# First attention of a four-layer kernel: probabilities normalised in ACT's cast, keys and values split on GpSimd, key halves placed by DMA

## The chip, the cores and the metric

One Trainium2 chip, one of its cores. The metric is the time of one execution on the device in microseconds; several executions are taken and their median is given. Engines are named as in the profile: PE (tensor engine, matmuls), ACT (scalar engine), DVE (vector engine), POOL (GpSimd), SP (the engine that issues most DMAs here).

## The reference, cut to what matters

Four layers, each followed by a residual sum and a layer norm: an attention with relative positions, a mixture of experts (top 2), a second attention, a second mixture with fixed capacity. The change is in the first, over 8 batches of 512 tokens of 128 features, 16 heads of 64:

```python
q, k, v = jnp.einsum('bsx,xAnh->Abnsh', input, w)
q = q + q_bias[:, None, :]
a = jnp.einsum('bnqh,bnkh->bnqk', q, k) * h ** (-0.5)
...
pos_scores = jnp.einsum('bnqh,nvh->bnqv', q, emb) * h ** (-0.5)
a = a + relative_causal(pos_scores)
mask = jnp.tril(jnp.ones((s, s), dtype=bool))
a = jax.nn.softmax(jnp.where(mask, a, NEG_INF), axis=-1)
o = jnp.einsum('bnqk,bnkh->bqnh', a, v).reshape(b, s, n * h)
...
out = o @ (out_kernel * (fan_in * fan_out) ** (-0.25)) + out_bias
```

## The kernel before, in words

The phase is `rel_attention_phase` (from L303). Each engine has its own program, and they meet by semaphores only. `schedule` (L333) gives every engine the same order: 64 bodies, one for each pair of heads n of a batch (8 pairs in each of 8 batches), with `k` alternating between 0 and 1 for double buffers; some bodies stand in loops over registers. The order within a body is written out by hand for each engine.

Products are taken in three float16 passes (high by high, low by high, high by low), so each operand is split: the high part is a cast to float16, the low part is the float32 value less the high part. The relative positions are folded into the score product: rows 0 to 63 of a head's 128 contraction rows are the head's q and k, rows 64 to 127 (for head 1 the other way round) hold fixed tables in `m.k_h`, `m.k_l` and projected q.

What a body does for the pair n, by engine:

- PE (`body` at L502): scores of head 0 (n) into three banks `score_ps`, projection of k for n+1 into `kv_ps`, projection of q of head 0 for n+1 into `q_ps`, `weighted_values` for n-2, scores of head 1, q of head 1, projection of v for n (again `kv_ps`), and the output projection for n-2. `weighted_values` (L458) first broadcasts the reciprocals of the row sums by eight float32 matmuls against the identity into `r_ps` (L466), then multiplies transposed probabilities and values (L476).
- ACT (L568): exponentials of head 0 with row sums (`exps`, L541), between them the copy of k out of PSUM with its scale (`k_copy`, L566), the cast of the unnormalised probabilities (128 x 1280) times `P_SCALE` to float16 (`high`, L550), the copy of `r_ps` (`r_copy`, L554), exponentials of head 1, the high part of v (`v_high`, L560), the cast of head 1.
- DVE (L644): maxima of head 0 (L594), reciprocals and low part of head 1 of the pair before (L602, L606), `q_evac` of head 0 for n+1 (bias and factor, L612), low part of head 0, `normalise` for n-2 (weighted values times reciprocals, L619), reciprocals of head 0, maxima of head 1, `q_evac` of head 1, low part of v (L623). At the last pair of a batch it adds the output bias to the residual (L628) and normalises the batch before (L123); at the third pair it sums that batch (L634).
- POOL (L711): four splits for n+1, in the order k of head 0 (64 partitions), q of head 0, k of head 1, q of head 1. A split is a one-column operation as a gate (L130), the high part (L691, an affine_select that writes float16) and the low part (L694). k is written into its 64 rows of `m.k_h` and `m.k_l`. At the last pair of a batch it computes the inverse deviation (L136, L137).
- SP (L406): issues the transposes of the float16 probabilities (`turn`, L404), head 1 of the pair before, then head 0 of this one, each when its low part is done.

Scores of head 1 wait for the exponentials of head 0 bank by bank, as the three score banks are shared, and those of head 0 for head 1's of the pair before. `kv_ps` is shared by k and v: the next k projection waits for `v_lo`, the v projection for `k_out`.

## Time and profile before

| what | value |
|---|---|
| median of 3 runs | 1677.52 us (1674.55 to 1745.03) |
| the profiled execution | 1676.82 us |
| its span in the profile | 1675.1 us |
| mean PE clock over the span | 0.948 of full |
| the first attention | from about 37 to 798 us of the span |

The profile has one record for each instruction. The page gives totals; windows give busy time within a stretch; the timeline gives instructions in order, with the idle time ahead of one and what released it in square brackets; waits are those idle times added up by waiter and releaser. "Busy" leaves out the time in which an instruction waits for a semaphore, but an instruction that has started and is held by something else counts as busy. Matmuls overlap in the records (their ends are modelled), so a busy PE need not be a saturated one. Times are us, means in the groups ns.

### The profile page before, as it was taken

How to read it: one execution, taken by the hardware profiler on the slowest of the kernel's cores; microseconds unless marked ns; L12 is line 12 of the kernel's file. 1: busy time of each engine (PE TensorE's matmuls, PEld its weight loads, DVE VectorE, ACT ScalarE, POOL GpSimd, SP SyncE). 2: the span in 40 equal slices, each digit the busy share in tenths (PEclk: the TensorE clock that was granted, in tenths of full speed). 3: DMA queues.
4: the chain of work that ended last, by engine and by line, in shares of the span. 5: the costliest groups of instructions: out<-in, count | busy, mean ns of one | idle time of the engine just before them, and what ended most of it. 6: DMA issues, size and time to landing. Idle time of an engine off the chain costs nothing. (4 is left out here: it accounts for less than half of the span.)

```text
span 1675.1 us, 38178 instructions
## 1 busy us (share of the span) xinstructions
PE 1421.9 (85%) x12519; PEld 834.2 (50%) x12519; DVE 1262.4 (75%) x2722; ACT 971.0 (58%) x1921; POOL 879.9 (53%) x1203
## 2 busy tenths in 40 slices
PE   4899989898998999897589887489899899898736
PEld 3566666666666666665356555123333333332216
DVE  3788888887888888886688888377787787777534
ACT  2677767676776767675244443156666666665431
POOL 2877778777787777775445555211221221222524
PEclk9899999999999999999699999599999999999977
DMA  5645545454454545544000000411011011010001
GB/s 160 123 113 127 123 98 125 97 122 110 110 125 105 114 111 118 116 110 94 0 2 0 0 0 0 146 48 35 27 39 36 26 39 36 26 40 28 13 12 27
DMA packets 372881, 116.47 MB, mean 70 GB/s; under 512 B 341675, under 2 KB 369312, under 8 KB 372704
## 3 DMA queue, kind: packets, MB, share of 16 engines
q1 hardware_dynamic: 369472, 111.36, 27.9%
q10 hardware_dynamic: 1824, 3.15, 0.6%
q0 software_dynamic: 1536, 1.34, 0.3%
q8 instruction: 27, 0.44, 0.1%
q14 instruction: 22, 0.18, 0.0%
HBM read 20.36 MB, written 12.89 MB: 20 GB/s over the span
## 5 line engine op out<-in xcount | busy, mean ns | idle before, releaser
L541 ACT ACTIVATE prob<-score_ps,nmax 128x512 f32<-128x512 f32 (+3 forms) x512 | 264.9, 526 | 209.0 <-DVE nmax L594 209.0
L1563 DVE TENSOR_REDUCE a_nm<-a_s 128x1 f16<-128x512 f32 x512 | 324.8, 687 | 55.5 <-PE a_s L1335 53.6
L1489 ACT ACTIVATE a_pt<-a_st 128x1024 f32<-128x1024 f32 x256 | 260.4, 1021 | 131.4 <-PE a_st L1353 116.3
L130 POOL TENSOR_TENSOR gate<-mhalf 128x1 f32<-128x1 f32 (+1 forms) x284 | 124.2, 437 | 259.3 <-ACT k L566 137.6
L1335 PE MATMUL a_s<-a_kop,a_qop 128*128 128x512 f16 x512 | 199.6, 391 | 64.2 <-DVE a_nm L1563 47.4
L606 DVE SCALAR_TENSOR_TENSOR p<-prob,p 128x1280 f16<-128x1280 f32 x128 | 204.6, 1598 | 49.8 <-ACT p L550 49.8
L594 DVE TENSOR_REDUCE nmax<-score_ps 128x1 f32<-128x512 f32 (+3 forms) x512 | 213.0, 475 | 3.4 <-PE score_ps L455 3.3
L452 PE MATMUL score_ps<-k_h,q_h 128*128 128x512 f16 (+3 forms) x512 | 158.2, 309 | 22.4 <-ACT prob L541 14.2
L550 ACT ACTIVATE p<-prob 128x1280 f16<-128x1280 f32 x128 | 163.8, 1279 | 6.5
L888 ACT ACTIVATE hid<-fps,b_cols 128x512 f32<-128x512 f32 x130 | 86.3, 687 | 127.2 <-PE fps L848 127.2
L694 POOL TENSOR_TENSOR q_l<-q,q_h 128x512 f16<-128x512 f32 x130 | 152.9, 1176 | 10.8
L454 PE MATMUL score_ps<-k_h,q_l 128*128 128x512 f16 (+3 forms) x512 | 156.9, 306 | 0.0
L453 PE MATMUL score_ps<-k_l,q_h 128*128 128x512 f16 (+3 forms) x512 | 156.7, 306 | 0.0
L694 POOL TENSOR_TENSOR k_l<-k,k_h 64x512 f16<-64x512 f32 x130 | 150.1, 1154 | 10.8
L1353 PE MATMUL a_st<-a_qop,a_kop 128*128 128x512 f16 x512 | 153.4, 383 | 0.2
L984 POOL TENSOR_TENSOR hid_l<-hid,hid_h 128x512 f16<-128x512 f32 x65 | 97.2, 1495 | 107.1 <-DVE hid_h L952 107.1
L1335 PEld LDWEIGHTS a_s<-a_kop,a_qop 128*128 128x128 f16 x512 | 50.8, 99 | 191.0 <-DVE a_nm L1563 156.0
L1366 PE MATMUL a_pv<-a_pt,a_vaug 128*32 128x512 f32 x1024 | 138.3, 612 | 0.7 <-ACT a_pt L1489 0.7
L476 PE MATMUL pv_ps<-pt,v_h 128*64 128x256 f16 (+1 forms) x1536 | 116.9, 256 | 0.3 <-DMA pt<-p 0.3
L455 PE MATMUL score_ps<-causal,ident_bf 128*128 128x128 bf16 x512 | 114.1, 223 | 0.0
L1685 POOL TENSOR_TENSOR a_vaug<-a_v,a_bv 128x128 f32<-128x128 f32 x32 | 14.4, 455 | 185.8 <-PE a_pv L1366 130.9
L862 PE MATMUL fps<-w_h,hid_h 128*128 128x128 f16 (+1 forms) x512 | 93.0, 221 | 21.0 <-POOL hid_l L984 19.4
(331 smaller groups left out, 3433.5 us busy)
## 6 DMA issues: line engine op xcount, KB each, us to landing
a_qop<-q_parts SPq DMA_DIRECT2D x32, 128.0 KB
a_kop<-k_parts SPq DMA_DIRECT2D x128, 24.0 KB
x_tok<-in_L_attn_input_dram SPq DMA_DIRECT2D x4, 512.0 KB, 12.3
pt<-p SPq DMA_TRANSPOSE x128, 4.1
e_w<-in_L_ffn_w_dram SPq DMA_DIRECT2D x1, 2048.0 KB, 8.3
q_parts<-a_q_h SPq DMA_DIRECT2D x16, 128.0 KB
k_parts<-a_k_h SPq DMA_DIRECT2D x16, 128.0 KB
out_dram<-a_res SPq DMA_DIRECT2D x8, 256.0 KB
```

The source lines that it names most:

```text
L452: nc.tensor.matmul(o, q_h[h][:, qs], m.k_h[h][:, 0:w], start=True, stop=False)
L453: nc.tensor.matmul(o, q_h[h][:, qs], m.k_l[h][:, 0:w], start=False, stop=False)
L454: nc.tensor.matmul(o, q_l[h][:, qs], m.k_h[h][:, 0:w], start=False, stop=False)
L541: ins = nc.scalar.activation(prob[h][:, P_OFF[c]:P_OFF[c] + w], score_ps[u][:, col:col + w], ACT.Exp, bias=nmax[h][:, c:c + 1], accum_out= ...
L550: nc.scalar.activation(p16[h][k][:, 0, :], prob[h][:, :], ACT.Copy, scale=P_SCALE).then_inc(p_hi[h], 1)
L594: ins = nc.vector.tensor_reduce(nmax[h][:, c:c + 1], score_ps[u][:, col:col + P * (c + 1)], AX.X, ALU.max, negate=True)
L606: nc.vector.scalar_tensor_tensor(p16[h][k][:, 1, :], prob[h][:, :], P_SCALE, p16[h][k][:, 0, :], ALU.mult, ALU.subtract).then_inc(p_lo[h], 1)
L694: return nc.gpsimd.tensor_tensor(lo, src, hi, ALU.subtract)
L1335: nc.tensor.matmul(s_ps[k][:, :], qop[:, g, c * P:(c + 1) * P], kop[:, hh, g, :], start=True, stop=True).then_inc(s_mm[k], 1)
L1353: mm = nc.tensor.matmul(st_ps[r][:, i, :], kop[:, 2 * r + i, g, kc * P:(kc + 1) * P], qop[:, g, :], start=True, stop=True)
L1489: nc.scalar.activation(pt[kc % 2][r][:, :, :], st_ps[r][:, :, :], ACT.Exp, scale=1.0 / SC).then_inc(exp_done[r], 1)
L1563: nc.vector.tensor_reduce(nm[g % 2][:, c, hh:hh + 1], s_ps[c % 2][:, :], AX.X, ALU.max, negate=True).then_inc(max_done[c % 2], 1)
```

## The change

`P_SCALE` becomes 64, and the probabilities are normalised before they are cast, so nothing is divided behind the weighted values:

- DVE's `reciprocals` also multiplies by `P_SCALE`, in an instruction of its own. ACT's `high` waits for it and casts in four pieces, one for each block of rows with its own factor per partition; DVE's `low` does the same in four pieces.
- The eight matmuls into `r_ps` go, and `normalise`; `r_copy` becomes `o_copy`, a copy of `pv_ps` to `o32`. The freed bank gives q a bank per head.
- `v_high` becomes `v_copy` (float32), and both parts of v are made on POOL (`split_v`). `v_low` goes.
- POOL splits the keys of both heads in one split of 128 partitions into `k16`, and SP places each half into `m.k_hl[h]` with a DMA (`place_k`), 64 partitions of 2 KB.
- The orders within a body change on ACT, DVE, POOL and SP. In the FFN phase one semaphore is saved.

```diff
-P_SCALE = 1024.0
+P_SCALE = 64.0
...
+            def place_k(h, n):
+                sp.wait_ge(k_split, n + 1)
+                sp.sem_inc(turn_open, 1)
+                sp.wait_ge(s_mm[h], 3 * n)
+                r = slice(64 * h, 64 * h + 64)
+                sp.dma_start(m.k_hl[h][r, :, :], k16[r, :, :]).then_inc(k_in[h], 16)
...
             def body(n, t, b, p, k):
                 if later(n, 1):
                     turn(1, n - 1, 1 - k)
+                place_k(0, n + 1)
                 turn(0, n, k)
+                place_k(1, n + 1)
...
             def scores(h, n):
                 pe.wait_ge(q_split[h], n + 1)
-                pe.wait_ge(k_split[h], n + 1)
+                pe.wait_ge(k_in[h], 16 * (n + 1))
...
             def high(h, n, t, k):
-                act.wait_ge(exp_done[h], count(n, 2))
+                act.wait_ge(r_done[h], n + 1)
                 if later(n, 2):
                     act.wait_ge(turned[h][k], 16 * t)
-                nc.scalar.activation(p16[h][k][:, 0, :], prob[h][:, :], ACT.Copy, scale=P_SCALE).then_inc(p_hi[h], 1)
+                for c in range(QC):
+                    cs = slice(P_OFF[c], P_OFF[c] + P * (c + 1))
+                    ins = nc.scalar.activation(p16[h][k][:, 0, cs], prob[h][:, cs], ACT.Copy, scale=rsum[h][:, c:c + 1])
+                ins.then_inc(p_hi[h], 1)
...
             def body(n, t, b, p, k):
-                exps(0, n, [0, 1])
+                exps(0, n, [0, 1, 2])
                 k_copy(n + 1)
-                exps(0, n, [2])
                 high(0, n, t, k)
                 if later(n, 2):
-                    r_copy(n - 2)
+                    o_copy(n - 2)
                 exps(1, n, [0, 1, 2])
-                v_high(n, k)
+                v_copy(n)
                 high(1, n, t, k)
...
-                nc.vector.reciprocal(rsum[k][:, :, h], sums[h][:, :]).then_inc(r_done[h], 1)
+                nc.vector.reciprocal(rsum[h][:, :], sums[h][:, :]).then_inc(r_steps, 1)
+                dve.wait_ge(r_steps, 2 * n + h + 1)
+                nc.vector.tensor_scalar(rsum[h][:, :], rsum[h][:, :], P_SCALE, None, ALU.mult).then_inc(r_done[h], 1)
...
-                nc.vector.scalar_tensor_tensor(p16[h][k][:, 1, :], prob[h][:, :], P_SCALE, p16[h][k][:, 0, :],
-                                               ALU.mult, ALU.subtract).then_inc(p_lo[h], 1)
+                dve.wait_ge(r_done[h], n + 1)
+                for c in range(QC):
+                    cs = slice(P_OFF[c], P_OFF[c] + P * (c + 1))
+                    ins = nc.vector.scalar_tensor_tensor(p16[h][k][:, 1, cs], prob[h][:, cs], rsum[h][:, c:c + 1], p16[h][k][:, 0, cs],
+                                                         ALU.mult, ALU.subtract)
+                ins.then_inc(p_lo[h], 1)
...
                 if later(n, 1):
-                    reciprocals(1, n - 1, 1 - k)
                     low(1, n - 1, 1 - k)
+                reciprocals(0, n)
                 q_evac(0, n + 1, pw)
                 if behind:
                     batch_stats(b - 1)
+                maxima(1, n)
                 low(0, n, k)
-                if later(n, 2):
-                    normalise(n - 2)
-                reciprocals(0, n, k)
-                maxima(1, n)
                 q_evac(1, n + 1, pw)
-                v_low(n, k)
+                reciprocals(1, n)
...
+            def split_k(n):
+                pool.wait_ge(k_out, n + 1)
                 for h in range(2):
-                    split_k(h, n)
-                    split_q(h, n)
+                    pool.wait_ge(k_in[h], 16 * n)
+                split(slice(0, P), k32[:, :], k16[:, 0, :], k16[:, 1, :], 4 * n + 1).then_inc(k_split, 1)
+
+            def split_v(n, k):
+                pool.wait_ge(v_out, n + 1)
+                if later(n, 2):
+                    pool.wait_ge(pv_mm, n - 1)
+                v = [t[k][:, :, :].rearrange("p c n -> p (c n)") for t in (v_h, v_l)]
+                split(slice(0, P), v32[:, :], v[0], v[1], 4 * n + 8).then_inc(v_split, 1)
...
             def body(n, t, b, p, k):
-                split_k(0, n + 1)
+                split_k(n + 1)
                 split_q(0, n + 1)
-                split_k(1, n + 1)
                 split_q(1, n + 1)
+                split_v(n, k)
```

## Rows read from the trace of the kernel before

**Rows 1.** The page: busy time, share and count of each engine over the span.

```profile
PE 1421.9 (85%) x12519; PEld 834.2 (50%) x12519; DVE 1262.4 (75%) x2722; ACT 971.0 (58%) x1921; POOL 879.9 (53%) x1203
```

**Rows 2.** Windows, one body: engine busy, then PE clock, DMA share, GB/s.

```profile
446.16:457.18 11.02, 10.50 (x115) 7.52 (x114) 9.00 (x17) 8.18 (x21) 8.67 (x13) 1.00 0.52 119
```

**Rows 3.** Waits in 100:740: waiter, releaser, total us, times, longest.

```profile
ACT prob L541 <- DVE nmax L594: 178.5, 111, 4.4
```

**Rows 4.** Timeline of DVE, one body: start, us, what, count [idle before].

```profile
445.44 1.67 DVE L594 TENSOR_REDUCE nmax<-score_ps 128x1 f32<-128x512 f32 x4
...
447.12 1.46 DVE L606 SCALAR_TENSOR_TENSOR p<-prob,p 128x1280 f16<-128x1280 f32 x1
...
450.21 1.69 DVE L606 SCALAR_TENSOR_TENSOR p<-prob,p 128x1280 f16<-128x1280 f32 x1 [0.97 <-ACT p L550]
...
452.51 1.65 DVE L594 TENSOR_REDUCE nmax<-score_ps 128x1 f32<-128x512 f32 x4
...
455.86 0.69 DVE L623 SCALAR_TENSOR_TENSOR v_l<-kv_ps,v_h 128x512 f16<-128x512 f32 x1 [1.05 <-ACT v_h L560]
456.47 0.68 DVE L594 TENSOR_REDUCE nmax<-score_ps 128x1 f32<-128x512 f32 x1
```

**Rows 5.** Timeline of ACT: key copies around a wrap, then one body.

```profile
398.97 0.60 ACT L566 ACTIVATE k<-kv_ps 128x512 f32<-128x512 f32 x1
...
414.20 0.60 ACT L566 ACTIVATE k<-kv_ps 128x512 f32<-128x512 f32 x1
...
447.74 0.60 ACT L566 ACTIVATE k<-kv_ps 128x512 f32<-128x512 f32 x1
...
448.91 1.27 ACT L550 ACTIVATE p<-prob 128x1280 f16<-128x1280 f32 x1
450.09 0.58 ACT L554 ACTIVATE r_sb<-r_ps 128x512 f32<-128x512 f32 x1
...
453.20 0.69 ACT L541 ACTIVATE prob<-score_ps,nmax 128x512 f32<-128x512 f32 x1 [2.53 <-DVE nmax L594]
...
455.22 0.61 ACT L560 ACTIVATE v_h<-kv_ps 128x512 f16<-128x512 f32 x1
```

**Rows 6.** Timeline of POOL, the same body: the operation ahead of a split.

```profile
448.57 0.19 POOL L130 TENSOR_TENSOR gate<-mhalf 64x1 f32<-64x1 f32 x1 [1.53 <-ACT k L566]
...
450.72 1.23 POOL L130 TENSOR_TENSOR gate<-mhalf 128x1 f32<-128x1 f32 x1 [0.17 <-POOL k_l L694]
```

**Rows 7.** Timeline of POOL and DVE at a wrap.

```profile
409.83 1.01 POOL L137 TENSOR_TENSOR ln_rstd<-ln_ve,mhalf 128x4 f32<-128x4 f32 x1
...
410.88 1.11 DVE L123 TENSOR_SCALAR x_tok<-ln_y,ln_mv,ln_rstd 128x128 f32 x4 [2.30 <-POOL ln_rstd L137]
```

**Rows 8.** Windows of line 466 alone, one body.

```profile
446.16:457.18 11.02, 1.09 (x16) 0.85 (x16) 1.00 0.52 119
```

**Rows 9.** Groups of ACT by form: count, busy us, mean ns, idle before.

```profile
L541 ACT ACTIVATE prob<-score_ps,nmax 128x512 f32<-128x512 f32 x128 | 87.9, 687 | 207.9 <-DVE nmax L594 207.9
...
L541 ACT ACTIVATE prob<-score_ps,nmax 128x128 f32<-128x128 f32 x128 | 46.6, 364 | 0.0
```

**Rows 10.** Timeline of POOL and DVE where they meet, and four pieces in a row.

```profile
438.37 1.15 POOL L694 TENSOR_TENSOR k_l<-k,k_h 64x512 f16<-64x512 f32 x1
...
438.71 2.16 DVE L606 SCALAR_TENSOR_TENSOR p<-prob,p 128x1280 f16<-128x1280 f32 x1 [0.37 <-ACT p L550]
...
799.54 3.75 POOL L990 TENSOR_SCALAR_AFFINE_SELECT w_h<-e_w 128x2048 f16<-128x2048 f32 x2 [1.46 <-SPq L733]
...
799.57 1.89 DVE L902 CAST wg_h<-wg_raw 128x8 f16<-128x8 f32 x1 [0.33 <-PEq L288]
...
870.87 1.12 DVE L961 SCALAR_TENSOR_TENSOR x_tok<-fps,comb,x_tok 128x128 f32 x4
```

**Rows 11.** DMA issues: tiles, queue, count, size, us to landing.

```profile
pt<-p SPq DMA_TRANSPOSE x128, 4.1
...
c_xe<-slot_rows SPq DMA_DIRECT2D x4, 162.5 KB, 3.8
```

More of the change, by code:

```diff
@@ L297, in rel_attention_phase @@
         k32 = sb("k32", [P, S], F32)
+        k16 = sb("k16", [P, 2, S], F16)
+        v32 = sb("v32", [P, S], F32)
         v_h = [sb(f"v_h{k}", [P, QC, P], F16) for k in range(2)]
@@ L306, in rel_attention_phase @@
         sums = [sb(f"sums{h}", [P, QC], F32) for h in range(2)]
-        rsum = [sb(f"rsum{k}", [P, QC, 2], F32) for k in range(2)]
+        rsum = [sb(f"rsum{h}", [P, QC], F32) for h in range(2)]
         y = sb("ln_y", [P, QC, D], F32)
@@ L313, in rel_attention_phase @@
         score_ps = [ps(f"score_ps{u}") for u in range(3)]
-        q_ps, kv_ps, pv_ps, r_ps, out_ps = ps("q_ps"), ps("kv_ps"), ps("pv_ps"), ps("r_ps"), ps("out_ps")
+        q_ps, pv_ps, out_ps = [ps(f"q_ps{h}") for h in range(2)], ps("pv_ps"), ps("out_ps")
+        kv_ps = ps("kv_ps")
         pair = lambda name: [sem(f"{name}{h}") for h in range(2)]
@@ L404, in turn, with first_front @@
                 sp.dma_start_transpose(pt[h][k][:, :, :], p16[h][k][:, :, :].rearrange("p a b -> p (a b)")).then_inc(turned[h][k], 16)
+            def place_k(h, n):
[4 more added lines that the diff above has]
+                sp.dma_start(m.k_hl[h][r, :, :], k16[r, :, :]).then_inc(k_in[h], 16)
+            def first_front():
+                place_k(0, 0)
+                place_k(1, 0)
             def body(n, t, b, p, k):
@@ L408, in body @@
                     turn(1, n - 1, 1 - k)
+                place_k(0, n + 1)
                 turn(0, n, k)
-            schedule(sp, lambda: None, body, lambda: turn(1, B * PAIRS - 1, 1))
+                place_k(1, n + 1)
+            schedule(sp, first_front, body, lambda: turn(1, B * PAIRS - 1, 1))
             sp.wait_ge(m.f0_loaded, m.F0_LOADS)
@@ L458, in weighted_values @@
             def weighted_values(n, t, k):
-                pe.wait_ge(r_done[1], n + 1)
                 if later(n, 1):
                     pe.wait_ge(o_done, n)
-                for c in range(QC):
-                    for h in range(2):
-                        nc.tensor.matmul(r_ps[64 * h:64 * h + 64, c * P:(c + 1) * P], rsum[k][:, c, h:h + 1].to_broadcast([P, 64]),
-                                         m.ident[:, :], start=True, stop=True)
-                pe.wait_ge(v_lo, n + 1)
+                pe.wait_ge(v_split, n + 1)
                 for h in range(2):
@@ L545, in high, with o_copy, v_copy @@
             def high(h, n, t, k):
[L547 removed]
+                act.wait_ge(r_done[h], n + 1)
                 if later(n, 2):
                     act.wait_ge(turned[h][k], 16 * t)
[L550 to L552 removed]
+                for c in range(QC):
+                    cs = slice(P_OFF[c], P_OFF[c] + P * (c + 1))
+                    ins = nc.scalar.activation(p16[h][k][:, 0, cs], prob[h][:, cs], ACT.Copy, scale=rsum[h][:, c:c + 1])
+                ins.then_inc(p_hi[h], 1)
+            def o_copy(n):
                 act.wait_ge(pv_mm, n + 1)
[L554 to L556 removed]
+                if later(n, 1):
+                    act.wait_ge(out_mm, n)
+                nc.scalar.activation(o32[:, :], pv_ps[:, :], ACT.Copy).then_inc(o_done, 1)
+            def v_copy(n):
                 act.wait_ge(v_mm, n + 1)
[L558 to L561 removed]
+                act.wait_ge(v_split, n)
+                nc.scalar.activation(v32[:, :], kv_ps[:, :], ACT.Copy, scale=W_SCALE).then_inc(v_out, 1)
             def k_copy(n):
                 act.wait_ge(k_mm, n + 1)
[L565 removed]
+                act.wait_ge(k_split, n)
                 nc.scalar.activation(k32[:, :], kv_ps[:, :], ACT.Copy, scale=W_SCALE * QK_SCALE).then_inc(k_out, 1)
             def body(n, t, b, p, k):
[L569 removed]
+                exps(0, n, [0, 1, 2])
                 k_copy(n + 1)
[L571 removed]
                 high(0, n, t, k)
                 if later(n, 2):
[L574 removed]
+                    o_copy(n - 2)
                 exps(1, n, [0, 1, 2])
[L576 removed]
+                v_copy(n)
                 high(1, n, t, k)
@@ L657, in body @@
                     batch_stats(b - 1)
+                maxima(1, n)
                 low(0, n, k)
-                if later(n, 2):
-                    normalise(n - 2)
-                reciprocals(0, n, k)
-                maxima(1, n)
                 q_evac(1, n + 1, pw)
-                v_low(n, k)
+                reciprocals(1, n)
                 if wrap:
@@ L676, in last @@
                 n = B * PAIRS
-                reciprocals(1, n - 1, 1)
                 low(1, n - 1, 1)
-                normalise(n - 2)
-                normalise(n - 1)
                 batch_sum(B - 1)
@@ L725, in last @@
                 layer_norm_gpsimd(nc, pool, m, B - 1, mv, ve, rstd)
-            schedule(pool, lambda: front(0), body, last)
+            schedule(pool, first_front, body, last)
 def moe_top2_phase(nc, io, m):
@@ L1980, in build @@
             m.wo = sb0("wo", [P, PAIRS, D], F32)
-            m.k_h = [sb0(f"k_h{h}", [P, S], F16) for h in range(2)]
-            m.k_l = [sb0(f"k_l{h}", [P, S], F16) for h in range(2)]
+            m.k_hl = [sb0(f"k_hl{h}", [P, 2, S], F16) for h in range(2)]
+            m.k_h, m.k_l = ([t[:, part, :] for t in m.k_hl] for part in range(2))
             m.q_mult = sb0("q_mult", [P, 2, S], F32)
```

66 lines of the change are left out of this document (21 added, 45 removed).

## The prediction

> **What bounds the kernel now.** The engine totals come first: no engine is full over the span, the tensor engine is nearest with 85% [rows 1]. They mix five phases, and the change lies in one, the first attention. So one of its bodies comes next: of 11.02 us PE is busy 10.50, DVE 9.00, ACT 8.18, POOL 8.67 (with PE's clock at 1.00 in this stretch) [rows 2]. In that phase the longest wait of all is ACT's for DVE's maxima [rows 3]. PE is fuller than the others, yet whether it sets the pace is not told by its share.
>
> The ring can be read off one body. DVE: maxima of head 0 from 445.44, low part of head 1 at 447.12, low part of head 0 at 450.21 after an idle 0.97 for ACT's cast, maxima of head 1 at 452.51, value low part at 455.86 after an idle 1.05 for ACT's value copy, next maxima at 456.47 [rows 4]. ACT: key copy 447.74, cast 448.91, exponentials of head 1 at 453.20, value copy 455.22 [rows 5]. So it runs DVE maxima, ACT exponentials with the key copy among them, ACT cast, DVE low and normalise, DVE maxima, ACT exponentials, value copy, DVE value low: 11.03 us, and DVE goes from one wait for ACT to the next. It is a ring of hand-overs between DVE and ACT; PE, 0.5 short of full, only fits into it. POOL needs 9.5 of the 11.02 and stands idle 1.53 before each key split [rows 6]. Once per batch a body takes 15.23 (key copies at 398.97 and 414.20) [rows 5]: DVE waits 2.30 for POOL's deviation and has a norm of 1.11 to do [rows 7]. The steady bodies start 11.02 or 11.03 apart.
>
> **The change part by part.** The sum is made against the profiled execution, 1676.8 (span 1675.1 and 1.7 around it), 0.7 under the median of 1677.5.
>
> *Removed from PE.* The sixteen passes that broadcast the reciprocals, 1.09 us per body [rows 8]. PE falls to about 9.4, so it is no bound under 9.4. Alone that is worth nothing, as PE isn't in the ring; bounds 0 and its wait-free share, 1.09.
>
> *Removed from DVE.* Normalise is what lies between the end of the low part at 450.21 (1.69 long) and the maxima at 452.51, 0.6 with a small reciprocal; the value low part is 456.47 less 455.86, 0.61 [rows 4]: 1.2 per body, both in the ring. The second q bank removes a cross wait that costs nothing now.
>
> *ACT's cast becomes four casts with a per-partition scale.* One cast of 1280 takes 1.27 [rows 5]: 1.08 is the stream (exponentials of 512 against 128 columns: 687 less 364 ns for 384, so 0.84 ns each [rows 9]), 0.2 is fixed. A per-partition operand costs 0.087 (exponential of 512 with its bias 687 [rows 9], key copy without one 600 [rows 5]). The cast at 448.91 is followed by the copy at 450.09, 0.09 before its end [rows 5], so pieces overlap by that. Four pieces: 1.08 + 4 x (0.2 + 0.087 - 0.09) = 1.9, plus 0.7 per head. Bounds: 1.38 if the fixed cost is paid once, 2.27 without overlap. I take 1.90, as the rows show each term. The Trainium skill ("ScalarE: Activation LUTs", section "What ACT_TABLE_LOAD costs") gives 186 ns fixed, 93 ns per pointer operand and 93 ns overlap back to back; by its figures the four would last 1.90, an estimate, and the rows agree.
>
> *DVE's low part becomes four.* The one instruction took 1.46 undisturbed (447.12) [rows 4], the next 0.08 before its end. Four scalar_tensor_tensors of 128 columns with pointer scalars take 1.12 at 870.87 [rows 10]: 0.27 each, 0.13 of it over a stream of about 1.04 ns a column (1.33 for 1280). So 1.33 + 4 x 0.13 = 1.85 instead of 1.38. Bounds 1.4 (nothing per piece) and 2.3 (the whole 0.27 over each).
>
> *Reciprocals.* A multiply and a self-wait are added, two each per body: some 0.4 instead of 0.1 to the release (three hand-overs and two instructions of 0.1 each; bounds 0.2 and 0.6); ACT now waits for it before each cast. On ACT the key copy or value copy (0.48) covers it if DVE is free.
>
> *The ACT ring without collisions.* Exponentials 2 x 2.02 (453.20 to 455.22), three copies of 0.48, two casts of 1.90, four hand-overs of 0.1: 4.04 + 1.44 + 3.80 + 0.40 = 9.7. DVE's work: maxima 2 x 1.6 (445.44 to 447.12, less a small reciprocal) [rows 4], low 2 x 1.85, q_evac 2 x 0.68 (what the 9.00 leaves for it), reciprocals 2 x 0.4 = 9.1. POOL: four splits as before (the second key's half is replaced by the value's), each 2.15 (448.57 to 450.72) [rows 6]: 8.6. So 9.7 would be the body, if nobody met anybody.
>
> *They do meet.* DVE's low part and POOL exclude each other, the whole instruction long. The low part at 438.71 took 2.16 instead of 1.46 because POOL's key low part ran until 439.52; a cast of eight columns took 1.89 behind POOL's select at 799.54 [rows 10]. The other way round POOL's gate took 1.23 instead of 0.19 behind the low part, 1.04 lost [rows 6]. Today one low part falls into POOL's 1.53 idle and only one collides. In the new order:
> - POOL's second q split needs q_evac(1), which DVE runs behind low(0); then comes the value split, 2.15 later. ACT's cast(1) starts 0.5 after q_evac(1) and lasts 1.90. So the value split starts just as low(1) does, always. Four pieces give POOL's 1.15 subtraction a boundary to enter at (DVE likewise gets in between two POOL operations at 799.57 [rows 10]); low(1) then ends after some 0.5 (the high part first) + 1.85 + 1.1 = 3.4, and reciprocals(0) behind it is 1.2 late against the exponentials' end at 2.1: plus 1.15.
> - The multiply in the reciprocals reads and writes SBUF alone, as the cast at 799.57 does, so it can wait for a POOL operation of up to 1.15. I take 0.3 per body, bounds 0 and 2.3.
> - Low(0) comes behind cast(0), while POOL splits key and q(0) without a pause; it waits for the rest of a 1.15 subtraction or is split by one: half of that and a little, plus 0.65, bounds 0 and 2.
>
> Body: 9.7 + 1.15 + 0.3 + 0.65 = 11.8, against 11.02. The Trainium skill ("SBUF — State Buffer", section "Who interferes with whom") says that a DVE instruction with two SBUF inputs contends with a GpSimd instruction that reads SBUF, and a one-source copy or tensor_scalar in a two-port mode as well, as an exclusive lock; the trace agrees for the low part (2.16 against 1.46), while no row has a tensor_scalar beside POOL. Without that rule the body would be 9.7 by the sum.
>
> *Keys by DMA.* Two more DMAs of 128 KB per body on SP's queue. A transpose lands 4.1 after its issue; place_k(0) is issued behind turn(1), place_k(1) behind turn(0). A plain DMA of 162.5 KB lands in 3.8 here [rows 11], which I take as the bound above.
>
> Half 0: key copy, 2.15 for the split, 3.8 for the DMA, so at most 6.0 after the key copy; scores and DVE's next maxima(0) come 0.9 later, and DVE gets there some 7.3 after the key copy. Hidden. Half 1: in a body that starts with the exponentials, low(0) ends at about 8.9, its transpose lands at 13.0, the half between 13.0 and 16.8. The next key split wants to start at 11.8 + 2.6 = 14.4. I take 14.0 (the DMA's way lies mostly beside the transpose), cost 0, bounds 0 and 2.4.
>
> *Batch edges.* Seven wraps. The deviation (1.01 and a small sum) [rows 7] now stands behind q(1) and the value split on POOL: 2 x 2.15 + 1.2 + 0.2 = 5.7 after q_evac(1), then DVE's norm 1.1 and the first maximum 0.7: exponentials 7.5 after q_evac(1), 2.4 in a plain body, plus 5.1. Statistics between q_evac(0) and maxima(1) put about 1.1 in the ring (taken as long as the norm). Together 6.2 over a body, now 15.23 - 11.02 = 4.2: plus 2.0 x 7 = 14; bounds 0 and 25.
>
> **Sum.** 63 steps between 64 bodies: 1676.8 + 63 x (11.8 - 11.02) + 14 = 1676.8 + 49 + 14 = **1740**. With every term at its lower bound PE's 9.4 would hold (about 1580), at the upper ones a body passes 14 (over 1850); neither end is likely in all terms at once.
>
> **The rivals.**
> - *Faster: the collisions mostly miss.* For it: 1.53 of idle on POOL today, and DVE's own 2.0. Against it: the value split is tied to low(1) by q_evac(1). Body 10.1 (9.7 and 0.4 for what is left): 1676.8 - 58 + 14 = 1633. Chance 0.25.
> - *Same: half of them.* The multiply isn't held and low isn't split by POOL: body 11.0, 1676.8 + 0 + 14 = 1690. Chance 0.2.
> - *My forecast*, body 11.8, own range 1705 to 1780. Chance 0.45.
> - *Slower still: key halves late.* Place: SP's queue behind turn(0). It decides once half 1 lands over 5.5 us behind the issue of that transpose (8.9 to 14.4); POOL's key split starts late and q, scores, maxima follow. At 6.5 the body is 12.8: 1676.8 + 112 + 14 = 1803. Chance 0.1.
>
> A measurement of this kernel can tell about 2%, 1644 and 1711. Faster 0.25, same 0.24 (the second rival and the lower edge of my range), slower 0.51. The range 1630 to 1800 takes in the first rival's time and ends short of the last's.
>
> **What would show it.** Right: bodies about 11.8 apart; the four casts 1.9 long; ACT waiting for reciprocals (DVE) ahead of casts; low pieces of over 1 us among shorter ones; POOL gates over 0.3; a wrap of 18. Wrong: bodies under 10.5 with ACT nearly full (no collisions), casts of 1.4 in sum (the fixed cost was mis-sized), or POOL's key gate waiting for a DMA (the keys' way is the bound).

## The result and the profile after

| what | before | after |
|---|---|---|
| median | 1676.16 us, 4 runs (1674.55 to 1745.03) | 1744.89 us, 4 runs (1743.88 to 1747.28) |
| ratio after/before | | 1.0415, 95% interval 1.0395 to 1.0436 |
| profiled execution, span | 1676.82, 1675.1 | 1747.28, 1745.6 |
| mean PE clock over the span | 0.948 | 0.934 |

The change makes the kernel 4.1% slower. 1740 was predicted, in a range of 1630 to 1800. The ratios leave out executions in a slower state of the chip: the 1745.03 above and one of 1984.39 in an experiment below.

The page of the changed kernel, its engine totals and the two groups that carry the new casts and low parts (count, busy us, mean ns of one, idle before):

```profile
PE 1370.0 (78%) x11495; PEld 785.6 (45%) x11495; DVE 1386.7 (79%) x3106; ACT 1046.7 (60%) x2305; POOL 823.0 (47%) x1201
...
L621 DVE SCALAR_TENSOR_TENSOR p<-prob,rsum,p 128x128 f16<-128x128 f32 (+3 forms) x512 | 364.3, 770 | 11.6 <-ACT p L563 11.6
...
L563 ACT ACTIVATE p<-prob,rsum 128x128 f16<-128x128 f32 (+3 forms) x512 | 245.6, 550 | 149.8 <-DVE rsum L614 149.8
```

Against [rows 1] PE has lost 52 us and DVE has gained 124, though it has shed `normalise` and the low part of v. The 512 low pieces take 770 ns in the mean, where four that nothing disturbs take 1.94 together (seen in two experiments below), under 500 each. So DVE's growth is in the low parts. ACT's casts are 550 ns in the mean, four of them 1.92 with their overlap, and 150 us of idle time stands ahead of them, all of it for DVE's `rsum`. Where ACT waited for DVE's maxima [rows 3], it now waits for the reciprocals:

The waits of the changed kernel from 100 to 780 us (waiter, releaser, total us, times, longest):

```profile
POOL gate L130 <- DVE q L628: 139.8, 56, 3.0
ACT p L563 <- DVE rsum L614: 129.0, 111, 2.1
...
PE score_ps L469 <- DMA k_hl<-k: 63.3, 78, 3.2
```

The first two are for DVE; the last one shown is for the keys' way over the DMA (PE's weight loads wait another 25.3 for them), and whether it matters is tried below. The window of one body answers to [rows 2] (its length, then busy time of PE, PE's weight loads, DVE, ACT and POOL, then clock, DMA share, GB/s):

```profile
472.26:483.95 11.69, 9.73 (x99) 6.65 (x97) 11.49 (x23) 9.34 (x28) 7.92 (x13) 1.00 0.61 136
```

The body has grown from 11.02 to 11.69, and DVE is busy 11.49 of it (11.03 to 11.45 in the next five), where it had been 9.00. Its timeline, one body from low part to low part, shows with what. A row of x4 holds four pieces and names the shape of the first:

```profile
472.39 3.21 DVE L621 SCALAR_TENSOR_TENSOR p<-prob,rsum,p 128x128 f16<-128x128 f32 x4 [0.37 <-ACT p L563]
...
475.71 0.51 DVE L614 TENSOR_SCALAR rsum<-rsum 128x4 f32<-128x4 f32 x1
...
478.39 2.74 DVE L621 SCALAR_TENSOR_TENSOR p<-prob,rsum,p 128x128 f16<-128x128 f32 x4
...
481.91 0.18 DVE L614 TENSOR_SCALAR rsum<-rsum 128x4 f32<-128x4 f32 x1
482.02 1.69 DVE L606 TENSOR_REDUCE nmax<-score_ps 128x1 f32<-128x512 f32 x4
```

POOL at the same time:

```profile
472.27 0.61 POOL L690 TENSOR_SCALAR_AFFINE_SELECT v_h<-v 128x512 f16<-128x512 f32 x1
472.97 1.16 POOL L693 TENSOR_TENSOR v_l<-v,v_h 128x512 f16<-128x512 f32 x1
475.08 0.56 POOL L130 TENSOR_TENSOR gate<-mhalf 128x1 f32<-128x1 f32 x1 [0.96 <-ACT k L580]
475.60 0.61 POOL L690 TENSOR_SCALAR_AFFINE_SELECT k<-k 128x512 f16<-128x512 f32 x1
...
481.88 0.19 POOL L130 TENSOR_TENSOR gate<-mhalf 128x1 f32<-128x1 f32 x1 [2.48 <-DVE q L628]
```

The reader is to see three things. The value split (472.27 to 474.13) stands inside the low part of head 1 (472.39 to 475.60), which takes 3.21. The low part of head 0 takes 2.74; it starts inside q's subtraction, which runs from 478.24 to 479.40. And the multiply at 475.71 takes 0.51 where its sister at 481.91 takes 0.18: it starts inside the select at 475.60 and ends with it. The same view over a window of 0.1 us gives single pieces:

```profile
472.95 1.45 DVE L621 SCALAR_TENSOR_TENSOR p<-prob,rsum,p 128x256 f16<-128x256 f32 x1
...
478.39 1.16 DVE L621 SCALAR_TENSOR_TENSOR p<-prob,rsum,p 128x128 f16<-128x128 f32 x1
```

Undisturbed these two take 0.48 and 0.35 (in the experiment with the thin value split, at 507.61 and 507.34). The first is the second piece of low(1), held while the value subtraction runs (472.97 to 474.13). The other is the first piece of low(0), held to the end of q's subtraction. So POOL enters low(1) at a boundary between two pieces, while low(0) only waits once, at its start.

With starts instead of lengths, since instructions overlap by 0.08, the body is: four undisturbed terms of DVE (maxima 2 x 1.59, low 2 x 1.86, q_evac 2 x 0.66, reciprocals 2 x 0.30) 8.82, waits and hand-overs 0.47, and 2.40 of collisions (1.26 in low(1), 0.81 in low(0), 0.33 in the multiply).

Once per batch, where [rows 7] show a wait of 2.30 for the deviation:

```profile
453.05 0.74 DVE L628 SCALAR_TENSOR_TENSOR q<-q_ps,q_bias,q_mult 128x512 f32<-128x512 f32 x1
...
459.41 1.12 DVE L123 TENSOR_SCALAR x_tok<-ln_y,ln_mv,ln_rstd 128x128 f32 x4 [4.24 <-POOL ln_rstd L137]
```

The wait is 4.24. The key copies tell the length of every step; here the first two, and the ones around this wrap:

```profile
38.21 0.60 ACT L580 ACTIVATE k<-kv_ps 128x512 f32<-128x512 f32 x1
70.03 0.60 ACT L580 ACTIVATE k<-kv_ps 128x512 f32<-128x512 f32 x1
...
445.90 0.59 ACT L580 ACTIVATE k<-kv_ps 128x512 f32<-128x512 f32 x1
463.19 0.61 ACT L580 ACTIVATE k<-kv_ps 128x512 f32<-128x512 f32 x1
474.27 0.60 ACT L580 ACTIVATE k<-kv_ps 128x512 f32<-128x512 f32 x1
485.96 0.59 ACT L580 ACTIVATE k<-kv_ps 128x512 f32<-128x512 f32 x1
```

The wrap is 17.29 (it was 15.24), the step behind it 11.08 and a plain one 11.69. The first step is 31.82, where the kernel before took 9.74: a loss that the prediction does not have. The queue of SP and DVE's first maximum say why:

```profile
36.92 1.45 SPq L366 DMA_DIRECT2D e_w<-in_L_ffn_W_dram  x2
...
60.70 0.43 SPq L380 DMA_DIRECT2D a_bo<-in_L_attn_bo_dram  x1
61.26 1.21 SPq L415 DMA_DIRECT2D k_hl<-k  x2
...
66.39 0.69 DVE L606 TENSOR_REDUCE nmax<-score_ps 128x1 f32<-128x512 f32 x1 [25.36 <-PE score_ps L472]
```

SP first issues the loads of later phases' weights, 24 us of them, and the halves of the first keys stand behind. DVE's first maximum comes at 66.39; before it came at 44.08.

From the first key copy to the last are 64 steps. They sum to 732.9 before and 801.8 after:

| steps | before | after | more | predicted |
|---|---|---|---|---|
| the first | 9.7 | 31.8 | 22.1 | 0 |
| the next 15 | 165.8 | 178.8 | 13.0 | 12 |
| 48 (six groups of eight, each with a wrap) | 557.4 | 591.2 | 33.8 | 49 |

### The profile page after: what moved, and what is told of

It reads as the page before. It is cut to its first block and busy times, and to the rows that moved or that the text cites. A ratio compares the mean times of both kernels' runs of the same rounds, so it can differ in the third digit from the quotient of the medians.

```text
span 1745.6 us, 37368 instructions
## 1 busy us (share of the span) xinstructions
PE 1370.0 (78%) x11495; PEld 785.6 (45%) x11495; DVE 1386.7 (79%) x3106; ACT 1046.7 (60%) x2305; POOL 823.0 (47%) x1201
## 3 DMA queue, kind: packets, MB, share of 16 engines
q0 software_dynamic: 1536, 1.34, 0.3%
## 5 line engine op out<-in xcount | busy, mean ns | idle before, releaser
L621 DVE SCALAR_TENSOR_TENSOR p<-prob,rsum,p 128x128 f16<-128x128 f32 (+3 forms) x512 | 364.3, 770 | 11.6 <-ACT p L563 11.6
L563 ACT ACTIVATE p<-prob,rsum 128x128 f16<-128x128 f32 (+3 forms) x512 | 245.6, 550 | 149.8 <-DVE rsum L614 149.8
L552 ACT ACTIVATE prob<-score_ps,nmax 128x512 f32<-128x512 f32 (+3 forms) x512 | 260.1, 516 | 61.4 <-DVE nmax L606 61.3
L469 PE MATMUL score_ps<-k_hl,q_h 128*128 128x512 f16 (+3 forms) x512 | 160.1, 313 | 145.2 <-DMA k_hl<-k 98.6
L130 POOL TENSOR_TENSOR gate<-mhalf 128x1 f32<-128x1 f32 x283 | 74.4, 263 | 387.6 <-DVE q L628 159.3
L471 PE MATMUL score_ps<-k_hl,q_l 128*128 128x512 f16 (+3 forms) x512 | 159.5, 312 | 0.0
L470 PE MATMUL score_ps<-k_hl,q_h 128*128 128x512 f16 (+3 forms) x512 | 159.4, 311 | 0.0
L469 PEld LDWEIGHTS score_ps<-k_hl,q_h 128*128 128x128 f16 x512 | 51.5, 101 | 193.6 <-ACT prob L552 91.5
L505 PE MATMUL out_ps<-wo,o 128*128 128x128 f32 (+1 forms) x512 | 74.5, 289 | 36.2 <-ACT o L570 36.1
```

Source lines behind the costliest of these rows:

```text
L469: nc.tensor.matmul(o, q_h[h][:, qs], m.k_h[h][:, 0:w], start=True, stop=False)
L470: nc.tensor.matmul(o, q_h[h][:, qs], m.k_l[h][:, 0:w], start=False, stop=False)
L471: nc.tensor.matmul(o, q_l[h][:, qs], m.k_h[h][:, 0:w], start=False, stop=False)
L552: ins = nc.scalar.activation(prob[h][:, P_OFF[c]:P_OFF[c] + w], score_ps[u][:, col:col + w], ACT.Exp, bias=nmax[h][:, c:c + 1], accum_out= ...
L563: ins = nc.scalar.activation(p16[h][k][:, 0, cs], prob[h][:, cs], ACT.Copy, scale=rsum[h][:, c:c + 1])
L621: ins = nc.vector.scalar_tensor_tensor(p16[h][k][:, 1, cs], prob[h][:, cs], rsum[h][:, c:c + 1], p16[h][k][:, 0, cs], ALU.mult, ALU.subtract)
```

## The experiments

All are built from the changed kernel, but for the last. They ran on chips on which the kernel before takes 1664.4 to 1665.2; there the changed kernel takes 1664.5 x 1.0415 = 1733.6 by its ratio. "Body" is the usual distance of key copies. Two theories stood against each other: the body is set by DVE's low parts and POOL's splits excluding each other (mine, with ACT's ring as the base); or by what was added as plain work (longer casts, more instructions), or by the keys' way over a DMA.

### The first keys ahead of the loads

```diff
+            place_k(0, 0)
+            place_k(1, 0)
             load(m.w1_raw[:, :, :], ...)
```

> The changed kernel with the first two key halves' DMAs issued ahead of SP's weight loads instead of behind them. Theory (first keys wait for SP's queue of loads at the start, where the first maxima come at 66.4 us instead of 44.1): the first maxima near 44, the second body still late since its keys stand behind the loads; in all 12 to 20 us less, about 1729. Rival (the start is covered later, as the loop catches up): no change. The steady body stays at 11.69 under both.

Measured: 1724.65, ratio 1.0365 (1.0334 to 1.0395), 9 less than the changed kernel. The first step is 9.45, but the second is 28.1: the second pair's key halves still stand behind the loads, which only moved the stall by a body. So the place was right, and what this edit gives was overrated. Spreading the loads comes below.

### q_evac of head 1 ahead of the low part of head 0

```diff
                 maxima(1, n)
+                q_evac(1, n + 1, pw)
                 low(0, n, k)
-                q_evac(1, n + 1, pw)
```

> The changed kernel with DVE's q_evac of head 1 ahead of the low part of head 0. Theory of collisions: POOL's second q split follows the first without a wait, the value split follows at the value copy and is over before the low part of head 1 starts; that low part falls from 3.2 to about 2 us, the body from 11.69 to 10.3 to 10.8, the time to 1660 to 1690. Rival (the four-piece casts and low parts alone make the ring longer, collisions cost nothing): body unchanged within 0.2, since the same instructions stand on every engine.

Measured: 1816.63, ratio 1.0917 (1.0886 to 1.0949), body 13.69; a miss. The low part of head 1 is indeed free now, but its neighbour and POOL are not. DVE and POOL of this kernel:

```profile
485.95 1.94 DVE L621 SCALAR_TENSOR_TENSOR p<-prob,rsum,p 128x128 f16<-128x128 f32 x4 [0.41 <-ACT p L563]
...
493.69 3.19 DVE L621 SCALAR_TENSOR_TENSOR p<-prob,rsum,p 128x128 f16<-128x128 f32 x4
```

```profile
488.65 0.19 POOL L130 TENSOR_TENSOR gate<-mhalf 128x1 f32<-128x1 f32 x1 [3.47 <-DMA k_hl<-k]
```

And its waits, from 100 to 780 us:

```profile
POOL gate L130 <- DMA k_hl<-k: 151.8, 43, 5.0
...
PE score_ps L469 <- DMA k_hl<-k: 131.6, 54, 4.4
```

The low part is 1.94 without company. But POOL waits up to 5.0 for a half of the keys: the half of head 1 is issued behind the transpose of head 0, that behind low(0), and low(0) is now later. That is the last rival of the prediction (key halves late), with a body of 13.7 instead of its 12.8. It does not hold in the changed kernel, where POOL waits for a key half 5 times in this window, 10.0 in all, but it is near.

### The value split cut to a thirty-second

```diff
-                split(slice(0, P), v32[:, :], v[0], v[1], 4 * n + 8).then_inc(v_split, 1)
+                pool_gate(nc, m, slice(0, P))
+                nc.gpsimd.affine_select(out=v[0][:, 0:16], in_=v32[:, 0:16], ...)
+                nc.gpsimd.tensor_tensor(v[1][:, 0:16], v32[:, 0:16], v[0][:, 0:16], ALU.subtract)
```

> The changed kernel with POOL's value split cut to 16 of 512 columns (the rest of both value parts stays zero, so 31/32 of the values are left out). Theory of collisions: the low part of head 1 no longer meets a 0.61 and a 1.15 us POOL operation, it falls from 3.2 to about 2, the body to 10.4 to 10.6, the time to about 1675. Rival (piece costs alone): body 11.6 to 11.7, the time within 10 us of 1745.

Measured: 1688.12 (one execution), body 11.06, 0.63 less; 10.4 to 10.6 had been expected, so a miss in size. DVE:

```profile
501.38 3.01 DVE L621 SCALAR_TENSOR_TENSOR p<-prob,rsum,p 128x128 f16<-128x128 f32 x4
...
507.34 1.94 DVE L621 SCALAR_TENSOR_TENSOR p<-prob,rsum,p 128x128 f16<-128x128 f32 x4 [0.37 <-ACT p L563]
```

Low(1) has fallen from 3.21 to 1.94, so the value split is what meets it, as predicted. The body got only half of the 1.27: low(0) has grown from 2.74 to 3.01, as the splits of key and q now lie otherwise against it, and 0.3 went into the maxima of head 1 (1.85 instead of 1.67) and waits ahead of q_evac.

### The low part in one instruction again

```diff
-                for c in range(QC):
-                    ...
-                    ins = nc.vector.scalar_tensor_tensor(p16[h][k][:, 1, cs], prob[h][:, cs], rsum[h][:, c:c + 1], ...)
-                ins.then_inc(p_lo[h], 1)
+                nc.vector.scalar_tensor_tensor(p16[h][k][:, 1, :], prob[h][:, :], rsum[h][:, 0:1], ...).then_inc(p_lo[h], 1)
```

> The changed kernel with DVE's low part in one instruction with the first block's factor for all four (so the low parts of three row blocks are computed with another block's factor). Theory of collisions: a whole instruction waits at most once for POOL and isn't entered by it; low parts of 1.5 to 2.6 us instead of 2.7 to 3.2, body 10.2 to 10.6, time about 1665. Rival (only the fixed cost per piece counts): 0.4 less per low part, body 10.9, time about 1695.

Measured: 1669.12 (one execution), bodies of 10.05 and 11.16 in turn, 10.61 in the mean: a hit. Two bodies' low parts:

```profile
483.96 2.33 DVE L619 SCALAR_TENSOR_TENSOR p<-prob,rsum,p 128x1280 f16<-128x1280 f32 x1
...
494.40 1.84 DVE L619 SCALAR_TENSOR_TENSOR p<-prob,rsum,p 128x1280 f16<-128x1280 f32 x1 [0.15 <-ACT p L563]
...
499.54 1.72 DVE L619 SCALAR_TENSOR_TENSOR p<-prob,rsum,p 128x1280 f16<-128x1280 f32 x1
```

In these two bodies it takes 1.72 to 2.36 where the four pieces took 2.74 and 3.21; over the run it takes 1.54 to 2.51. Two things come off: the three more pieces (0.40 per low part, 1.94 against the 1.54 of a whole one that meets nobody, as at 72.42), and POOL's entries between them; each low part still meets POOL, but once. The body gains 1.08 of some 1.8 that the two low parts lose, as DVE now waits for others (its maxima at 482.19 for PE, 1.12).

This run also shows a reciprocal and the multiply behind it, both beside one subtraction of POOL (74.52 to 75.67):

```profile
74.54 0.17 DVE L612 RECIPROCAL rsum<-sums 128x4 f32<-128x4 f32 x1
...
74.74 0.95 DVE L614 TENSOR_SCALAR rsum<-rsum 128x4 f32<-128x4 f32 x1
```

The multiply is held to the end of the subtraction, the reciprocal is not.

### The cast in one instruction again

```diff
-                for c in range(QC):
-                    ...
-                    ins = nc.scalar.activation(p16[h][k][:, 0, cs], prob[h][:, cs], ACT.Copy, scale=rsum[h][:, c:c + 1])
+                nc.scalar.activation(p16[h][k][:, 0, :], prob[h][:, :], ACT.Copy, scale=rsum[h][:, 0:1])
```

> The changed kernel with ACT's cast in one instruction with the first block's factor for all four (the high parts of three row blocks get another block's factor). The cast falls from 1.92 to about 1.37. If ACT sets the pace, the body falls by 1.1 to 10.6 (time 1676). If DVE with its waits for POOL sets it (it is busy 11.49 of 11.69 with those waits counted), the casts lie beside DVE's work and the body falls by 0.6 or less, time 1708 to 1745.

Measured: 1719.21 (one execution), body 11.39 in the mean, 0.3 less. ACT and DVE of it:

```profile
485.82 1.36 ACT L561 ACTIVATE p<-prob,rsum 128x1280 f16<-128x1280 f32 x1 [1.42 <-DVE rsum L611]
```

```profile
482.07 2.75 DVE L618 SCALAR_TENSOR_TENSOR p<-prob,rsum,p 128x128 f16<-128x128 f32 x4
...
487.52 3.18 DVE L618 SCALAR_TENSOR_TENSOR p<-prob,rsum,p 128x128 f16<-128x128 f32 x4
```

The two casts have become 2 x 0.56 shorter and the body 0.3, which is about the 0.37 that DVE had stood idle for a cast. The low parts are as long as before, and ACT stands idle 1.42 ahead of a cast. So ACT's casts are not what sets the body; DVE is. This is what had been expected of that case (0.6 or less).

### Without the multiply

```diff
-                nc.vector.reciprocal(rsum[h][:, :], sums[h][:, :]).then_inc(r_steps, 1)
-                dve.wait_ge(r_steps, 2 * n + h + 1)
-                nc.vector.tensor_scalar(rsum[h][:, :], rsum[h][:, :], P_SCALE, None, ALU.mult).then_inc(r_done[h], 1)
+                nc.vector.reciprocal(rsum[h][:, :], sums[h][:, :]).then_inc(r_done[h], 1)
```

> The changed kernel without the multiply of the reciprocals and without the wait ahead of it (the probabilities are scaled by 1 instead of 64). The two instructions and waits take 0.2 to 0.5 each. Theory: body 11.69 less 0.4 to 0.7, time about 1705 to 1720. Rival (they lie beside ACT's copies): body unchanged.

Measured: 1710.56 (one execution), 23 less, bodies of 11.2 to 11.3: a hit. Two multiplies had cost 0.2 each in plain work and the one 0.33 more when held; 0.48 of it comes off a plain body, 0.40 off the mean of the 48 steps.

### The second key half ahead of the transpose

```diff
                 place_k(0, n + 1)
+                place_k(1, n + 1)
                 turn(0, n, k)
-                place_k(1, n + 1)
```

> The changed kernel with SP issuing the second key half ahead of the transpose of head 0 instead of behind it. PE waited 88.6 us in all for the key halves in the window 100:780. Theory (these waits are covered, PE isn't in the ring): time within 5 us of 1745, and PE's waits for the keys nearly gone. Rival (keys' way is in the ring): body 0.5 to 1 shorter, time 1685 to 1715.

Measured: 1733.38, ratio 1.0414 (1.0393 to 1.0435), body 11.71. The wait, from 100 to 780 us:

```profile
PE score_ps L469 <- DMA k_hl<-k: 34.8, 38, 2.2
```

PE's wait for keys falls from 63.3 to 34.8, that of its weight loads goes from 25.3 to 28.3, and the time does not move. The time is a hit, but the waits were expected to be nearly gone, and 63.1 of 88.6 are left. They are covered too: DVE, which sets the body, stands idle for scores only 8.2 in this window of the changed kernel. So the rival of late keys is out.

### Loads spread, with q_evac early

The loads of later phases are queued, eight behind each of the first bodies, and the first keys are placed ahead of all; q_evac as above.

```diff
-                sp.dma_start(dst, src, ...).then_inc(m.a_loaded, 16)
+                queued.append((dst, src, scattered))
...
                 place_k(1, n + 1)
+                for _ in range(8):
+                    if queued:
+                        dst, src, scattered = queued.pop(0)
+                        sp.dma_start(dst, src, ...).then_inc(m.a_loaded, 16)
```

> Both mends: the first key halves ahead of SP's loads, with the loads of the second attention's weights spread over four bodies of the first batch, and DVE's q_evac of head 1 ahead of the low part of head 0. If both costs are as the theory has them and add up: 1745 less 22 less about 65, so 1650 to 1665, under the kernel before by 1%. Rival (the ring closes elsewhere, at PE or at the low parts): 1680 to 1720.

Measured: 1799.78, ratio 1.081 (1.0788 to 1.0832), body 13.67: a miss in the body, with POOL's wait of the second experiment (147.4 for key halves in 100 to 780, 42 times), and its first steps 10.43 and 12.12: the stall at the start is gone.

### The same with both key halves ahead of the transpose

> The changed kernel with q_evac of head 1 ahead of low part 0 (as in k2), and also both key halves issued ahead of the transpose of head 0 and the weight loads spread over the first bodies. In k2 POOL waited 3.5 us per body for a key half that stood behind that transpose. If that is what made k2 slow (body 13.7), here the wait goes and the body is 10.4 to 11.2, the time 1630 to 1690. Rival (the earlier q_evac itself makes it slow, since POOL's q split now enters low part 0 and DVE waits for q): body over 12, time over 1750.

Its edit is the sum of the two before. Measured: 1711.74, by one execution. Bodies of 11.65 and 12.25, a miss for both theories. POOL's wait for key halves is gone (PE still waits 48.3 for them, from 100 to 780 us), so it was what made the two runs with early q slow; but the body is not 10.4 to 11.2, because low(0) now stands where the splits are densest:

```profile
544.71 3.77 DVE L625 SCALAR_TENSOR_TENSOR p<-prob,rsum,p 128x128 f16<-128x128 f32 x4
...
551.10 1.94 DVE L625 SCALAR_TENSOR_TENSOR p<-prob,rsum,p 128x128 f16<-128x128 f32 x4 [0.41 <-ACT p L567]
```

```profile
545.44 0.24 POOL L130 TENSOR_TENSOR gate<-mhalf 128x1 f32<-128x1 f32 x1
545.64 0.86 POOL L694 TENSOR_SCALAR_AFFINE_SELECT q_h<-q 128x512 f16<-128x512 f32 x1
546.59 1.34 POOL L697 TENSOR_TENSOR q_l<-q,q_h 128x512 f16<-128x512 f32 x1
547.89 0.64 POOL L130 TENSOR_TENSOR gate<-mhalf 128x1 f32<-128x1 f32 x1
```

POOL's gate, select and subtraction (0.24, 0.86 and 1.34 against 0.19, 0.61 and 1.16 elsewhere) run in turn with the four pieces. The collision was moved from one low part to the other, not removed. By the next run, q_evac in its old place would give about 1711 here (an estimate: 1687.65 and the 23 of the multiply), so the earlier q_evac is worth nothing. Why the bodies alternate between two lengths was not found out.

### Loads spread, no multiply

```diff
-P_SCALE = 64.0
+P_SCALE = 1.0
```

with the edits of spread loads, early halves and no multiply as above, and q_evac where the change put it.

> The changed kernel with the loads of the second attention's weights spread over four bodies and the first keys ahead of them, both key halves ahead of the transpose, and the multiply of the reciprocals gone with the probabilities' scale set to 1 everywhere. Costs add up if they are apart: 1733 (this chip) less 22 for the start, less 23 for the multiply, 0 for the key halves: 1688, bodies of 11.2. Rival (the start's delay only moves into later bodies, as in k1): about 1700 to 1710.

Measured: 1687.65, ratio 1.0141 (1.0121 to 1.0161), first steps 9.44 and 10.72, body 11.20: a hit to the microsecond. From 1733.5 that is 46 less: 23 are the multiply's (measured alone), so 23 are the start's, against the 22.1 of the table.

### Keys and values on POOL, probabilities as before

The parts of the change without the normalisation: cast, low, `normalise` and the broadcast of the reciprocals as in the kernel before; loads spread.

```diff
             def high(h, n, t, k):
-                for c in range(QC): ...
+                nc.scalar.activation(p16[h][k][:, 0, :], prob[h][:, :], ACT.Copy, scale=P_SCALE)
...
+                nc.vector.tensor_tensor(o32[:, :], pv_ps[:, :], r_sb[:, :], ALU.mult)
```

> The other parts of the change alone: keys of both heads in one split and placed by DMA (ahead of the transposes, loads spread), values split on POOL, but probabilities cast unnormalised in one piece, low parts in one piece, reciprocals broadcast on PE and applied by DVE as before, with one bank for q. DVE loses only the value low part (0.61). If the value low part's 0.6 and the value copy's 0.5 leave the ring and PE (10.5 busy) is next: body 10.5, time 1630 to 1640 against 1665 before. Rival (the value split meets the second low part on the shared path and gives it back): body 11.0 to 11.3, time 1660 to 1680. Either way the normalisation is the part that costs.

Measured: 1685.8, ratio 1.0132 (1.0105 to 1.0158), body 11.36, wrap 16.8. The rival was right in kind and too small: it had 11.0 to 11.3 and at most 1680. POOL of this kernel:

```profile
504.60 2.28 POOL L708 TENSOR_TENSOR v_l<-v,v_h 128x512 f16<-128x512 f32 x1
...
508.80 1.44 POOL L130 TENSOR_TENSOR gate<-mhalf 128x1 f32<-128x1 f32 x1
```

The value subtraction takes 2.28 instead of 1.16, held by the low part at 503.94, and POOL then runs two more splits without a pause. So the value split on POOL costs 0.3 per body and, against the keys alone (below, wrap 14.2), 2.5 per wrap, even with whole low parts.

### The keys alone

From the kernel before: one split of both heads' keys, the halves placed by DMA ahead of the transpose of head 0, the loads spread. Nothing else is changed.

```diff
-                split_k(0, n + 1)
+                split_k(n + 1)
                 split_q(0, n + 1)
-                split_k(1, n + 1)
                 split_q(1, n + 1)
```

> The kernel before with only the keys changed: one split of both heads' keys on POOL, halves placed by DMA ahead of the transposes, weight loads spread over the first bodies. Values, casts, low parts and normalisation as before. POOL has three splits per body instead of four. Theory (POOL's value split, which meets the low parts on the shared path and stands ahead of the deviation, is what made k11 lose 0.34 per body and more at the wraps): steady bodies stay at 11.02, the ring of DVE and ACT being untouched; at the wraps DVE's wait of 2.3 for POOL's deviation falls by one split of 2.15, so 7 x 2 = 15 less, time 1650 against 1665 before: this would beat both kernels. Rival (the keys' way through SP and DMA is what cost k11): body 11.2 to 11.4, time 1680 to 1690.

Measured: 1661.41 (12 runs, 1657.73 to 1663.82) against 1664.48 (17 runs), ratio 0.998 (0.9972 to 0.9989). It is 0.2% faster than the kernel before, and 4.2% faster than the changed one. Body 11.03, as before, which rules out the rival that the keys' way costs; wrap 14.22 instead of 15.24; the first eight steps, among which the loads now stand, cost 4.6 more in sum. The expected 1650 is missed: 3 came off instead of 15. DVE and POOL at its wrap:

```profile
408.51 0.73 DVE L631 SCALAR_TENSOR_TENSOR q<-q_ps,q_bias,q_mult 128x512 f32<-128x512 f32 x1
...
413.05 1.12 DVE L123 TENSOR_SCALAR x_tok<-ln_y,ln_mv,ln_rstd 128x128 f32 x4 [1.19 <-POOL ln_rstd L137]
```

```profile
409.32 0.19 POOL L130 TENSOR_TENSOR gate<-mhalf 128x1 f32<-128x1 f32 x1 [1.14 <-DVE q L631]
...
411.27 0.65 POOL L136 TENSOR_TENSOR ln_ve<-ln_mv,ln_eps 128x4 f32<-128x4 f32 x1
```

Of the 2.15 that the removed split is worth, 1.0 arrives: POOL now waits 1.14 for q_evac(1), so the rest of the split had stood beside DVE's work anyway, and the sum of the deviation takes 0.65 where it took 0.20. In the plain body the ring of [rows 4, 5] does not hold a split, so a POOL that waits 2.7 for the key copy gives nothing.

These runs part the 69 us into pieces (estimates, as they compare runs by their times alone). From the kernel before, 1664.5, keys with the loads spread give 3 back (1661.4). Values on POOL cost 24 (1685.8). The normalisation, with its orders and the second bank for q, costs 25 (to 1710.6, which is 1687.65 and the 23 of the multiply; the multiply is 23 of these 25). The first keys behind the loads cost 23 (1733.6).

## Why the prediction was right, and where it was not

*Casts: right.* 1.90 was taken, 1.92 measured (four pieces in a row); a piece of 512 is 706 ns and one of 128 is 402. The Trainium skill ("ScalarE: Activation LUTs", section "What ACT_TABLE_LOAD costs") gave the same 1.90 as an estimate, and the trace agrees.

*Low part without company: right.* 1.85 was predicted, 1.86 from start to start measured. The whole low part with the same pointer scalar takes 1.54, so three boundaries cost 0.40, and 0.13 for each is what the prediction took.

*The value split is tied to low(1): right.* It begins at 472.27, low(1) at 472.39. The prediction let it cost 1.15, and low(1) is 1.26 longer: 0.29 in its first piece, beside the value's select, and 0.97 in its second, which waits while the subtraction has entered at the boundary. Making the split thin takes it off. What the prediction missed is that this is no separate price: where a split is taken away, POOL's others move, and low(0) took a fifth of it back.

*Low(0): right.* 0.65 predicted, 0.81 measured, all of it in the first piece: of the two ways that the prediction named, it waits for the rest of a subtraction and is not split by one.

*The multiply: its mechanism right, its size low.* 0.3 was predicted for the hold and 0.33 is seen in the body above; 53 of the 128 multiplies take 0.51 or 0.52, those that are not held 0.17 or 0.18. But its plain 0.2 was thought hidden behind ACT's copies, and on a full DVE nothing is hidden: leaving the multiply out gives 0.48 per plain body and 23 us. The Trainium skill ("SBUF — State Buffer", section "Who interferes with whom") names tensor_scalar among those that can take the pair shared with GpSimd; the held multiply agrees: all 53 start inside a select of POOL. The reciprocals of this kernel never meet a select or a subtraction; in the run with whole low parts 57 of them start inside one and take 0.16 to 0.18, so they are not held.

*ACT's ring as the base: wrong.* "So 9.7 would be the body, if nobody met anybody" stands on ACT; the body stands on DVE, which is busy 11.49 of 11.69. Its own terms are 8.82 and 0.47 of waits, 9.3, and 2.40 of collisions on top make 11.69. The prediction took 9.7 and 2.1. The two errors nearly cancel, and the whole-cast run shows which base is right: with 1.1 less on ACT the body lost 0.3.

*Keys by DMA, cost 0: right in the body, wrong at the start.* Placing the halves earlier changed nothing, so the way is covered; they land in 2.3, inside the bounds. But the first halves stand behind SP's loads, and that costs 22. The prediction reckoned the queue of a steady body only, and never asked what SP issues as the phase begins, although it names SP's queue as the place of the late-keys rival.

*Batch edges: right in the mechanism.* Norm 5.7 after the end of q_evac(1) was predicted: 453.8 to 459.4 are 5.6. The step is 17.28 instead of the 18.0, and the 0.6 that the step behind the wrap gains was not foreseen, nor that the body with the batch's sum, already 11.50 before, would grow by 0.2 only (the sum falls where DVE waits for a cast). Therefore 49 predicted against 34 measured in those 48 steps.

*The sum.* 63 was forecast and 70.5 came in the span, 69 of it in the 64 steps: the 22 of the start is missing in the forecast, the rest (48 measured) is 15 too high, and the two mostly cancel. So 1740 is right by its main mechanism, and by some luck to within 0.3%. The rivals of missed collisions, 1633 and 1690, asked for bodies of 10.1 and 11.0 and are out; the kernel comes near the second with the multiply out and the loads spread (1687.65), or with a thin value split (1688.12).

*Small terms.* The rows of the kernel before show POOL's 1.53 of idle time ahead of head 0's key split only, not ahead of each. A split takes 1.95 of POOL's time in the changed body, where 2.15 was taken, and PE is busy 9.73 instead of 9.4. None of the three moves the sum, as neither engine sets the body.

Left open: why the kernel with q and key halves early alternates between 11.65 and 12.25, and what the change would give with normalised casts but no split of values on POOL; the thin split hints at the latter, 1688 with the start's 22 still in it, so about the time of the kernel before.

## What to carry to other kernels

A DVE instruction with two SBUF inputs that runs beside a busy GpSimd should stay in one piece: a boundary can let a GpSimd operation in (four pieces took 3.21 and 3.77 where that happened, 1.94 undisturbed; a whole one took 1.54 to 2.51), and moving the meeting point to another place only changes which one pays. When an operand gets a DMA on its way, look at what that queue issues when the phase begins, not in the steady body alone. Work that is moved to the engine with idle time is only free if that engine's later outputs (here the deviation at each wrap) are not awaited, and gains only if it leaves the ring: of this change, the merged key split with spread loads alone was shown to be worth having, and its gain is 0.2%.

## What was not expected of the hardware

- POOL and DVE take turns, instruction by instruction: in the kernel with q and key halves early, gate, select and subtraction each lengthened (0.24, 0.86, 1.34 against 0.19, 0.61, 1.16) while the four pieces took 3.77 against 1.94. The prediction had let POOL in once per low part.
- A multiply over 128 x 4 elements takes 0.51 instead of 0.18 when it starts inside a select of POOL, and 0.95 inside a subtraction, while a reciprocal of the same size inside that subtraction takes 0.17.
- The low part in one piece takes 1.54 with a pointer scalar and 1.46 with an immediate, both undisturbed, so the pointer costs 0.08 here; in four pieces it takes 1.94.
- Swapping two DVE instructions made the body 2 us longer, through the order of a DMA queue, while POOL's wait for that DMA is 10.0 of 680 us in the changed kernel.
